# A gated-attention stage in another order of issue: context projection between the feed-forward's products, its norm ahead of the sum, one quarter of the squares on ScalarE

## The chip, the core and the metric

The kernel runs on one core of a Trainium2 chip. The metric is the device time of one execution in microseconds; the median of three runs is used. All data are fp32 except where bf16 is said.

## The reference, cut to what matters

The whole program is eight residual layers over `x` of shape 8 x 512 x 128. The change touches the stage between the fifth layer's attention and the seventh layer's attention. That stage computes, for each of the 8 batches:

```python
x = x + context @ W_o.T                      # end of the fifth layer
h = layernorm(x) @ W_fc' ; r = relu(h)**2    # sixth layer: 512 hidden columns, in 4 quarters
x = x + r @ W_proj'
n = layernorm(x)                             # seventh layer: gated attention, its inputs
q, k, v = n @ wq + bq, n @ wk + bk, n @ wv + bv
c = tanh(q @ wfq + bfq + mean(q) @ wfg + bfg)
p, z = c @ up, c @ uz                        # per head: position and steepness of a curve
```

The curve from `p` and `z`, and `q` and `k`, are split into three bf16 parts each and stored to DRAM, from where the seventh layer's attention loads them.

## The kernel before

The stage is the class `GatedPhase`. It is a software pipeline over 8 batches (`NB`), one batch per step, each batch spread over five steps: in step `s` the code works on batch `s` ("lag 0"), `s-1`, `s-2`, `s-3` and `s-4`. There is no scheduler at run time. Each engine has its own list, written out by hand in the methods `tensor`, `scalar`, `vector`, `vector_late` and `gpsimd`, executes it strictly in that order, and waits on semaphores where data come from another engine. `store` is the list of the DMA queue SP.

A batch goes this way. Lag 0: `out.project` (L173, TensorE), `out.add` (L179, VectorE adds it to `x`), `norm.statistics` and `aggregate_alone` (L213, L238, VectorE), `scale_alone` (L244, L247, GpSimd), `normalise_alone` (L254, VectorE), `norm.turn` (L269, transposes on TensorE), `norm.copy` (L275, ScalarE). Lag 1: `ffn.hidden` four times (L403, TensorE; the quarters in the order 2, 0, 3, 1), `ffn.relu` (L408, ScalarE) and `ffn.square` (L413) of each quarter, `ffn.project` (L421, 32 instructions on TensorE, which needs all four squares), `ffn.add` (L428, VectorE), then the second norm by the same lines as the first, `query` (L675), `key` (L679), `mix_query` (L692), `globals` (L730). Lag 2: `centre` (L725), `centre_tanh` (L743), `steepness` (L748), `value` (L684), `position` (L752), `values` (L719), and the splits of q and k into parts (`query_high`, `query_rest` L703, `middle` L452, `low` L456). Lag 3: `steep` (L759 exponential, L762 square, ScalarE), `position_tanh`, `distance`, `curves` (L779, L781, VectorE), `curves_high` (L786), `curves_rest` (L791). Lag 4: the last split of the curve (`c_split.low`, L456 with 1536 columns) and its stores (L1253 to L1259).

In the kernel before, squares 0 and 1 are on VectorE and squares 2 and 3 on GpSimd. GpSimd's list for step `s` holds `ffn.square(pool, s, ...)`, so it waits there for the relus of the next step.

PSUM has eight banks, and `Banks` gives each product one of them by a table; the entry of a table row is (name, bank, lag, semaphores of its readers). `take` makes TensorE wait until the bank's user before has been read. Before, `o` (the feed-forward's sum) and `out` (the context's) share bank 1, so `out.project` waits for `ffn.add` of the batch before.

In `last_group` further work is put between the steps: `rest.scale` on GpSimd in step 2 (L1428), and fills of the attention's operand stacks (L1571 on GpSimd, L1712 on VectorE, L1727 on ScalarE) with the attention's loads on SP (L1515) after steps 7, 8 and 10. TensorE leaves the stage after step 9 and enters the attention.

Of the kernel before, what the change touches and what calls it, by code (L numbers as in the profile page):

```python
# [11 lines left out]
ACT = mybir.ActivationFunctionType  # L12
# [74 lines left out]
def batch(s, lag):  # L87

    return (s - lag,) if 0 <= s - lag < NB else ()


class Banks:
# [4 lines left out]
    def __init__(self, nc, tag, count, plan, tensors=None, prior=None):  # L97
        self.tensors = tensors if tensors is not None else [nc.alloc_psum_tensor(f"{tag}_bank{i}", [P, 512], F32) for i in range(count)]
        self.prior = prior
        self.where = {name: bank for name, bank, _, _ in plan}  # L100
        self.readers = {name: readers for name, _, _, readers in plan}
        self.before, last = {}, {}
        uses = sorted((b + lag, k, name, bank, b) for k, (name, bank, lag, _) in enumerate(plan) for b in range(NB))
        for _, _, name, bank, b in uses:
            self.before[name, b] = last.get(bank)
            last[bank] = (name, b)
        self.last = last
# [54 lines left out]
class OutProjection:  # L162
# [6 lines left out]
    def project(self, pe, b):  # L169
        self.context.context_done(pe, b)  # L170
        to = self.banks.take(pe, "out", b)
        for t in range(NT):
            last = pe.matmul(to[:, t * D:(t + 1) * D], self.sv.ctxT[:, b, t * P:(t + 1) * P], self.wo, start=True, stop=True)  # L173
        last.then_inc(self.projected, 1)
# [213 lines left out]
class SquaredRelu:  # L388
# [21 lines left out]
    def square(self, eng, b, k):  # L410
        eng.wait_ge(self.relu_done[k], b + 1)
        r = self.r[b % 2][:, k, :]
        eng.tensor_tensor(r, r, r, ALU.mult).then_inc(self.sq_done[k], 1)  # L413

    def project(self, pe, b):
        for k in range(NK):
# [110 lines left out]
def x_tiles_of(tensor, b):  # L527

    return tensor[:, b * NT:(b + 1) * NT, :]
# [264 lines left out]
class PolarPhase:  # L794
# [44 lines left out]
    def tensor(self, pe, s):  # L839
        norm, norm2, ffn, prep = self.norm, self.norm2, self.ffn, self.prep  # L840
        for b in batch(s, 3):
            ffn.combine(pe, b)
        for b in batch(s, 4):
            norm2.turn(pe, b)
            prep.project(pe, b)
            prep.value(pe, b)
        for b in batch(s, 1):
            ffn.route(pe, b)
        for b in batch(s, 0):
            norm.turn(pe, b)  # L850
        for b in batch(s, 2):
            ffn.turn(pe, b)
        for b in batch(s, 1):
            ffn.low_rank(pe, b)
# [77 lines left out]
    def gpsimd(self, pool, s):  # L932
        norm, norm2, ffn, prep = self.norm, self.norm2, self.ffn, self.prep
        for b in batch(s, 5):
            norm2.scale(pool, b)
        for b in batch(s, 3):
            ffn.bias(pool, b)
        for b in batch(s, 0):
            norm.scale(pool, b)
# [151 lines left out]
class GatedPhase:  # L1091
# [4 lines left out]
    def __init__(self, nc, sv, tag, wo, early, late, psum, context):  # L1096
        self.sv = sv
        out = self.out = OutProjection(early, sv, f"{tag}_o", wo, context)
        ffn_norm = Norm(early, sv, f"{tag}_n", "xnT", out.added)
        ffn = self.ffn = SquaredRelu(early, sv, f"{tag}_f", ffn_norm, last_hidden=1)  # L1100
        norm, norm2 = self.norm, self.norm2 = ffn_norm, Norm(early, sv, f"{tag}_m", "xnT2")
        prep = self.prep = PrepareGated(late, sv, f"{tag}_p", norm2, early)
        norm2.x_ready = ffn.x_done
        self.place = (4, 5, 6, 7, 0, 1, 2, 3)
        banks = self.banks = Banks(nc, tag, 8, (
            ("h2", 4, 1, (ffn.relu_done[2],)), ("h0", 2, 1, (ffn.relu_done[0],)), ("h3", 5, 1, (ffn.relu_done[3],)), ("h1", 3, 1, (ffn.relu_done[1],)),
            ("c", 5, 2, (prep.cT_ready,)), ("o", 1, 1, (ffn.x_done,)), ("out", 1, 0, (out.added,)),
            ("z", 6, 2, (prep.ez_ready,)), ("v", 4, 2, (prep.v_ready,)), ("p", 7, 2, (prep.th_ready,)), ("xnT2", 0, 1, (norm2.xnT_ready,)),
            ("q", 2, 1, (prep.q_ready,)), ("xnT", 0, 0, (norm.xnT_ready,)), ("k", 3, 1, (prep.k_split.rest_ready,)), ("g", 5, 1, (prep.gb_ready,))), tensors=[psum[:, i, :] for i in self.place])
        out.banks = norm.banks = norm2.banks = ffn.banks = prep.banks = banks  # L1110

    def bank_done(self, eng, place):
# [22 lines left out]
    def tensor(self, pe, s):  # L1135
        out, norm, norm2, ffn, prep = self.out, self.norm, self.norm2, self.ffn, self.prep
        for b in batch(s, 1):
            ffn.hidden(pe, b, 2)
            ffn.hidden(pe, b, 0)
            ffn.hidden(pe, b, 3)  # L1140
            ffn.hidden(pe, b, 1)
        for b in batch(s, 2):
            prep.centre(pe, b)
        for b in batch(s, 1):
            ffn.project(pe, b)
        for b in batch(s, 0):
            out.project(pe, b)
        for b in batch(s, 2):
            prep.steepness(pe, b)
            prep.value(pe, b)  # L1150
            prep.position(pe, b)
        for b in batch(s, 1):
            norm2.turn(pe, b)
            prep.query(pe, b)
        for b in batch(s, 0):
            norm.turn(pe, b)
        for b in batch(s, 1):
            prep.key(pe, b)
            prep.globals(pe, b)

    def scalar(self, act, s):
        out, norm, norm2, ffn, prep = self.out, self.norm, self.norm2, self.ffn, self.prep
        for b in batch(s, 2):
            prep.query_high(act, b)
            prep.key_high(act, b)
        for b in batch(s, 3):
            prep.steep(act, b)
        for b in batch(s, 1):
            ffn.relu(act, b, 2)
            ffn.relu(act, b, 0)  # L1170
            ffn.relu(act, b, 3)
            ffn.relu(act, b, 1)
        for b in batch(s, 3):
            prep.position_tanh(act, b)
            prep.distance(act, b)
        for b in batch(s, 2):
            prep.centre_tanh(act, b)
            prep.q_split.middle(act, b)
            prep.k_split.middle(act, b)
        for b in batch(s, 3):  # L1180
            prep.curves_high(act, b)
        for b in batch(s, 4):
            prep.c_split.middle(act, b)
        for b in batch(s, 1):
            norm2.copy(act, b)
            prep.mix_query(act, b)
        for b in batch(s, 0):
            norm.copy(act, b)

    def vector_start(self, dve):  # L1190
        out, norm, norm2, ffn, prep = self.out, self.norm, self.norm2, self.ffn, self.prep
# [2 lines left out]
    def vector(self, dve, s):  # L1194
        out, norm, norm2, ffn, prep = self.out, self.norm, self.norm2, self.ffn, self.prep
        for b in batch(s, 2):
            prep.global_bias(dve, b)
            prep.key_rest(dve, b)
        for b in batch(s, 1):
            ffn.square(dve, b, 0)  # L1200
            ffn.square(dve, b, 1)
        for b in batch(s, 2):
            prep.query_rest(dve, b)
        for b in batch(s, 3):
            prep.curves(dve, b)
        for b in batch(s, 2):
            prep.q_split.low(dve, b)
            prep.k_split.low(dve, b)
        for b in batch(s, 1):
            ffn.add(dve, b)  # L1210
            norm2.statistics(dve, b)
            norm2.aggregate_alone(dve, b)
        for b in batch(s, 0):
            out.add(dve, b)
            norm.statistics(dve, b)
            norm.aggregate_alone(dve, b)
        for b in batch(s, 1):
            norm2.normalise_alone(dve, b)
        for b in batch(s, 2):
            prep.values(dve, b)  # L1220
        for b in batch(s, 0):
            norm.normalise_alone(dve, b)

    def vector_late(self, dve, s):
        prep = self.prep
# [4 lines left out]

    def gpsimd(self, pool, s):
        out, norm, norm2, ffn, prep = self.out, self.norm, self.norm2, self.ffn, self.prep
        for b in batch(s, 1):
            norm2.scale_alone(pool, b)
        for b in batch(s, 0):
            norm.scale_alone(pool, b)
            ffn.square(pool, b, 2)
            ffn.square(pool, b, 3)

    def store(self, sp, s):  # L1240
        sv, prep = self.sv, self.prep
# [1838 lines left out]
```

## Time and profile before

| | |
|---|---|
| median of 3 runs | 1714.1 us (1712.29 to 1714.25) |
| the profiled execution | 1712.71 us, its span 1710.9 us |
| busy over the span | PE 1504.7 us, DVE 1190.1, ACT 1257.0, POOL 530.2 |
| the gated stage | from 1111 us (first `out.project`) to 1300 us (the attention's reductions run without a stop) |
| one steady step of it | 18.33 us |
| TensorE's granted clock, mean | 0.95 of full speed |

PE is TensorE's matmuls, PEld its weight loads, DVE VectorE, ACT ScalarE, POOL GpSimd, SP the queue of transfers. L numbers are lines of the kernel. PEclk is the granted TensorE clock as a share of 2.4 GHz. In a timeline, a line's start minus the start of the line before it on the same engine is what the instruction occupies when the engine does not wait; the duration shown is some 0.1 us longer, since the next instruction starts before the last one's results are all written.

### The profile page before, as it was taken

How to read it: one execution, taken by the hardware profiler on the slowest of the kernel's cores; microseconds unless marked ns; L12 is line 12 of the kernel's file. 1: busy time of each engine (PE TensorE's matmuls, PEld its weight loads, DVE VectorE, ACT ScalarE, POOL GpSimd, SP SyncE). 2: the span in 40 equal slices, each digit the busy share in tenths (PEclk: the TensorE clock that was granted, in tenths of full speed). 3: DMA queues.
4: the chain of work that ended last, by engine and by line, in shares of the span. 5: the costliest groups of instructions: out<-in, count | busy, mean ns of one | idle time of the engine just before them, and what ended most of it. 6: DMA issues, size and time to landing. Idle time of an engine off the chain costs nothing. (4 is left out here: it accounts for less than half of the span.)

```text
span 1710.9 us, 37885 instructions
## 1 busy us (share of the span) xinstructions
PE 1504.7 (88%) x14142; PEld 724.0 (42%) x14142; DVE 1190.1 (70%) x1933; ACT 1257.0 (73%) x2113; POOL 530.2 (31%) x908
## 2 busy tenths in 40 slices
PE   7889987774699999998889999978874999999998
PEld 4666666662133333336633333345541333333356
DVE  4778777798999999967710000047878999999743
ACT  4654563697488888885689999926663888888863
POOL 3422342552323333334400010022221333333362
PEclk9999998797699999999999999989986999999999
DMA  4000000025434444420133333211333333333211
GB/s 132 1 1 2 1 2 1 1 82 166 142 102 111 107 110 111 107 62 27 45 89 98 94 100 97 66 36 39 99 108 113 84 91 89 89 92 92 67 38 38
DMA packets 140411, 125.42 MB, mean 73 GB/s; under 512 B 38411, under 2 KB 118341, under 8 KB 140229
## 3 DMA queue, kind: packets, MB, share of 16 engines
q1 hardware_dynamic: 130980, 121.90, 24.6%
q0 software_dynamic: 8192, 0.77, 0.9%
q8 instruction: 113, 1.85, 0.5%
q14 instruction: 70, 0.57, 0.1%
q10 hardware_dynamic: 1056, 0.33, 0.1%
HBM read 77.19 MB, written 44.96 MB: 71 GB/s over the span
## 5 line engine op out<-in xcount | busy, mean ns | idle before, releaser
L1700 ACT ACTIVATE m_probs<-m_psum 128x512 f32<-128x512 f32 (+1 forms) x768 | 511.6, 761 | 60.9 <-PE m_psum L1623 59.9
L1700 ACT ACTIVATE e_probs<-e_psum 128x512 f32<-128x512 f32 x512 | 276.4, 596 | 53.6 <-PE e_psum L1623 52.0
L1740 DVE TENSOR_REDUCE a_minus_max<-m_psum 128x2 f32<-128x1024 f32 x256 | 300.8, 1218 | 14.4 <-PE m_psum L1632 13.1
L1740 DVE TENSOR_REDUCE a_minus_max<-e_psum 128x2 f32<-128x1024 f32 x256 | 300.5, 1218 | 14.8 <-PE e_psum L1632 13.3
L1623 PE MATMUL m_psum<-m_q_stack,m_k_stack 114*32 114x512 bf16 (+1 forms) x4096 | 294.3, 384 | 6.6 <-DMA m_k_stack<-n_parts 4.4
L1643 PE MATMUL m_psum<-m_probs,m_v_ones 128*32 128x512 f32 x2048 | 269.5, 599 | 3.9 <-DVE m_pair L1690 2.6
L1623 PEld LDWEIGHTS m_psum<-m_q_stack,m_k_stack 114*32 114x32 bf16 (+1 forms) x4096 | 106.4, 96 | 224.2 <-issue 124.6
L1623 PE MATMUL e_psum<-e_q_stack,e_k_stack 126*32 126x512 bf16 x2048 | 157.5, 384 | 2.3 <-ACT e_probs L1700 2.2
L1643 PE MATMUL e_psum<-e_probs,e_v_ones 128*32 128x512 f32 x1024 | 132.2, 593 | 0.0
L1632 PE MATMUL m_psum<-m_k_stack,m_q_stack 48*128 48x512 bf16 x512 | 93.2, 400 | 31.8 <-DVE a_minus_max L1740 24.3
L1632 PE MATMUL e_psum<-e_k_stack,e_q_stack 60*128 60x512 bf16 x512 | 93.9, 400 | 29.4 <-DVE a_minus_max L1740 23.6
L1583 POOL CAST a_max_parts<-a_minus_max 128x16 bf16<-128x16 f32 x64 | 12.7, 198 | 325.2 <-DVE a_minus_max L1740 325.2
L1522 POOL DMA_DIRECT2D m_q_stack<-a_max_rows x128 | 76.6, 604 | 58.5 <-DVE a_max_rows L1745 51.3
L1522 POOL DMA_DIRECT2D e_q_stack<-a_max_rows x128 | 76.4, 603 | 57.8 <-DVE a_max_rows L1745 50.8
L1623 PEld LDWEIGHTS e_psum<-e_q_stack,e_k_stack 126*32 126x32 bf16 x2048 | 43.8, 95 | 117.1 <-ACT e_probs L1700 70.0
L1962 POOL TENSOR_TENSOR s_rope_product<-s_qkv,rope 128x512 f32<-128x512 f32 x32 | 40.2, 1287 | 152.3 <-ACT s_qkv L1927 152.3
L1643 PEld LDWEIGHTS m_psum<-m_probs,m_v_ones 128*32 128x32 f32 x2048 | 52.4, 109 | 78.9 <-ACT m_probs L1700 53.2
L1577 POOL COPY m_v_ones<-vtok 128x128 f32<-128x128 f32 x64 | 18.6, 292 | 213.2 <-PE m_psum L1643 213.2
L1690 DVE COPY slot_w<-m_psum 128x512 f32<-128x512 f32 x8 | 5.5, 691 | 111.8 <-PE m_psum L1643 111.8
L1413 DVE RECIPROCAL slot_wo<-slot_wo 128x64 f32<-128x64 f32 x24 | 13.1, 546 | 91.1 <-DMA slot_wo<-a_context_pairs 91.1
L1632 PEld LDWEIGHTS m_psum<-m_k_stack,m_q_stack 48*128 48x128 bf16 x512 | 24.6, 93 | 114.5 <-issue 53.3
L1632 PEld LDWEIGHTS e_psum<-e_k_stack,e_q_stack 60*128 60x128 bf16 x512 | 24.5, 93 | 114.3 <-DVE a_minus_max L1740 53.8
(402 smaller groups left out, 2630.3 us busy)
## 6 DMA issues: line engine op xcount, KB each, us to landing
polar_q<-m_late SPq DMA_DIRECT2D x24, 256.0 KB, 3.0
polar_k<-m_late SPq DMA_DIRECT2D x24, 256.0 KB, 3.2
m_q_stack<-polar_q SPq DMA_DIRECT2D x64, 96.0 KB, 2.3
m_k_stack<-polar_k SPq DMA_DIRECT2D x64, 96.0 KB, 2.4
ctx<-a_context_pairs SPq DMA_DIRECT2D x48, 128.0 KB
a_context_pairs<-slot_w SPq DMA_DIRECT2D x24, 256.0 KB, 2.2
m_q_stack<-dist_parts SPq DMA_DIRECT2D x192, 32.0 KB
m_k_stack<-dist_parts SPq DMA_DIRECT2D x192, 32.0 KB
```

What stands on the lines that cost most here:

```text
L1413: dve.reciprocal(self.inverse, self.sums).then_inc(self.inverted, 1)
L1522: pool.dma_start(rows[:, :, j:j + 32], self.max_rows[j:j + 32, :]).then_inc(self.rows_loaded, 16)
L1577: pool.tensor_copy(self.buf.v_ones[n % 2][:, :, :, DH * (n % 2):DH * (n % 2) + DH], self.sv.vtok[:, tiles_of(b), :].rearrange("p t (h d) - ...
L1583: pool.tensor_copy(self.max_parts[:, 0, :], self.minus_max[n % 2][:, :]).then_inc(self.hi_ready, 1)
L1623: last = pe.matmul(self.ps_s[i % self.PAIRS][r:r + 32, j, :], self.buf.k_stack[g][0:self.rows, h, c * P + r:c * P + r + 32], self.buf.q_st ...
L1632: pe.matmul(to[:, :], self.buf.q_stack[g][part, h, t * P:(t + 1) * P], self.buf.k_stack[g][part, h, :], start=True, stop=True).then_inc(se ...
L1643: last = pe.matmul(self.ps_pv[32 * h:32 * h + self.buf.VW, :], self.buf.v_ones[m % 2][:, c, h, :], self.buf.probs[(NT * m + c) % self.buf. ...
L1690: copied = eng.tensor_copy(self.buf.pair[k % 2][:, :], self.ps_pv[:, :])
L1700: act.activation(self.buf.probs[(NT * m + c) % self.buf.PROBS][:, self.WIDE * part:self.WIDE * (part + 1), :], self.ps_s[i % self.PAIRS], ...
L1740: dve.tensor_reduce(self.minus_max[n % 2][:, k:k + NT + 1:NT], self.ps_r[r % self.TWOS], AX.X, ALU.max, negate=True).then_inc(self.two_fre ...
L1962: pool.tensor_tensor(self.products[n][:, :, :, :], halves[:, :, :, i, :], table, ALU.mult).then_inc(self.rope_steps, 1)
```

## The change

`out` moves to bank 0, which it shares with `xnT` and `xnT2`; `o` has bank 1 alone. TensorE issues `out.project` (batch s) between `ffn.hidden` and `centre`, and `norm.turn` (batch s) directly after `ffn.project`. VectorE issues `out.add`, its statistics and its aggregation directly after its squares, `normalise_alone` of that norm after `curves`, hence ahead of `ffn.add`; `k_split.low` and `values` go behind the second norm's aggregation. Square 3 moves from GpSimd to VectorE, square 2 to ScalarE; GpSimd keeps the norms' scales alone. ScalarE issues `steep` behind its third relu and `norm.copy` ahead of `norm2.copy`.

```diff
+    def square_beside(self, act, b, k):
+        act.wait_ge(self.relu_done[k], b + 1)
+        r = self.r[b % 2][:, k, :]
+        act.activation(r, r, ACT.Square).then_inc(self.sq_done[k], 1)
...
-            ("c", 5, 2, (prep.cT_ready,)), ("o", 1, 1, (ffn.x_done,)), ("out", 1, 0, (out.added,)),
+            ("out", 0, 0, (out.added,)), ("c", 5, 2, (prep.cT_ready,)), ("o", 1, 1, (ffn.x_done,)), ("xnT", 0, 0, (norm.xnT_ready,)),
...
-            ("q", 2, 1, (prep.q_ready,)), ("xnT", 0, 0, (norm.xnT_ready,)), ("k", 3, 1, (prep.k_split.rest_ready,)), ("g", 5, 1, (prep.gb_ready,))), tensors=[psum[:, i, :] for i in self.place])
+            ("q", 2, 1, (prep.q_ready,)), ("k", 3, 1, (prep.k_split.rest_ready,)), ("g", 5, 1, (prep.gb_ready,))), tensors=[psum[:, i, :] for i in self.place])
...
@@ tensor
             ffn.hidden(pe, b, 1)
+        for b in batch(s, 0):
+            out.project(pe, b)
         for b in batch(s, 2):
             prep.centre(pe, b)
         for b in batch(s, 1):
             ffn.project(pe, b)
         for b in batch(s, 0):
-            out.project(pe, b)
+            norm.turn(pe, b)
...
-        for b in batch(s, 0):
-            norm.turn(pe, b)
-        for b in batch(s, 1):
             prep.key(pe, b)
...
@@ scalar
+        for b in batch(s, 1):
+            ffn.relu(act, b, 2)
+            ffn.relu(act, b, 0)
+            ffn.square_beside(act, b, 2)
+            ffn.relu(act, b, 3)
         for b in batch(s, 3):
             prep.steep(act, b)
         for b in batch(s, 1):
-            ffn.relu(act, b, 2)
-            ffn.relu(act, b, 0)
-            ffn.relu(act, b, 3)
             ffn.relu(act, b, 1)
...
+        for b in batch(s, 0):
+            norm.copy(act, b)
         for b in batch(s, 1):
             norm2.copy(act, b)
             prep.mix_query(act, b)
-        for b in batch(s, 0):
-            norm.copy(act, b)
@@ vector
             ffn.square(dve, b, 0)
+            ffn.square(dve, b, 3)
             ffn.square(dve, b, 1)
+        for b in batch(s, 0):
+            out.add(dve, b)
+            norm.statistics(dve, b)
+            norm.aggregate_alone(dve, b)
         for b in batch(s, 2):
             prep.query_rest(dve, b)
         for b in batch(s, 3):
             prep.curves(dve, b)
+        for b in batch(s, 0):
+            norm.normalise_alone(dve, b)
         for b in batch(s, 2):
             prep.q_split.low(dve, b)
-            prep.k_split.low(dve, b)
         for b in batch(s, 1):
             ffn.add(dve, b)
             norm2.statistics(dve, b)
             norm2.aggregate_alone(dve, b)
-        for b in batch(s, 0):
-            out.add(dve, b)
-            norm.statistics(dve, b)
-            norm.aggregate_alone(dve, b)
+        for b in batch(s, 2):
+            prep.k_split.low(dve, b)
+            prep.values(dve, b)
         for b in batch(s, 1):
             norm2.normalise_alone(dve, b)
-        for b in batch(s, 2):
-            prep.values(dve, b)
-        for b in batch(s, 0):
-            norm.normalise_alone(dve, b)
@@ gpsimd
+        for b in batch(s, 0):
+            norm.scale_alone(pool, b)
         for b in batch(s, 1):
             norm2.scale_alone(pool, b)
-        for b in batch(s, 0):
-            norm.scale_alone(pool, b)
-            ffn.square(pool, b, 2)
-            ffn.square(pool, b, 3)
```

## Rows read from the trace of the kernel before

**Rows 1.** Busy time by stretch: gated stage, step 0 to 1, 1 to 2, one steady step.
```profile
core 0: us, PE busy (x) PEld busy (x) DVE busy (x) ACT busy (x) POOL busy (x), PEclk, DMA share, GB/s
1130.60:1150.25 19.65, 15.22 (x64) 9.45 (x64) 10.75 (x35) 8.57 (x14) 4.61 (x6) 0.83 0.05 16
1205.43:1223.76 18.33, 15.68 (x76) 9.84 (x76) 16.19 (x39) 12.01 (x20) 5.02 (x6) 1.00 0.32 93
```

**Rows 2.** Timeline, TensorE, one steady step: start, us, engine, line, operation, [idle before <- releaser].
```profile
1194.86 3.70 PE L403 MATMUL e_psum<-e_v_ones,ffn_fc 128*128 128x512 f32 x8
1200.84 3.81 PE L421 MATMUL e_psum<-ffn_proj,e_probs 128*128 128x128 f32 x32 [0.99 <-DVE e_probs L413]
1205.43 1.16 PE L173 MATMUL e_psum<-l1a_wo,ctx 128*128 128x128 f32 x8 [0.78 <-DVE x L428]
1206.42 1.02 PE L748 MATMUL e_psum<-e_probs,l1b_up 128*128 128x512 f32 x2
1209.04 0.98 PE L269 MATMUL e_psum<-ident,e_q_stack 128*128 128x128 f32 x4
1210.71 1.13 PE L675 MATMUL e_psum<-e_k_stack,l1b_w 128*128 128x512 f32 x2 [0.69 <-ACT e_k_stack L275]
1213.19 3.70 PE L403 MATMUL e_psum<-e_k_stack,ffn_fc 128*128 128x512 f32 x8
```

**Rows 3.** Timeline, VectorE, the same step.
```profile
1200.66 0.68 DVE L703 SCALAR_TENSOR_TENSOR e_late<-pope_table,e_late 128x512 f32<-128x512 f32 x1
1201.26 0.68 DVE L779 TENSOR_TENSOR e_late<-e_late 128x512 f32<-128x512 f32 x1
1202.58 1.28 DVE L456 TENSOR_TENSOR e_late<-e_late 128x512 bf16<-128x512 f32 x2
1204.68 0.69 DVE L428 TENSOR_TENSOR x<-e_psum,x 128x512 f32<-128x512 f32 x1 [0.81 <-PE e_psum L421]
1205.41 0.87 DVE L213 BATCH_NORM_STATS2 e_pair<-x 128x6 f32<-128x128 f32 x4
1206.32 0.38 DVE L238 BATCH_NORM_AGGREGATE e_pair<-e_pair 128x2 f32<-128x6 f32 x4
1208.55 1.08 DVE L254 TENSOR_SCALAR e_q_stack<-x,e_pair 128x128 f32<-128x128 f32 x4
1209.56 0.68 DVE L719 TENSOR_TENSOR vtok<-e_psum,bv 128x512 f32<-128x512 f32 x1
```

**Rows 4.** Timeline, ScalarE and GpSimd, the same step.
```profile
1195.78 0.61 ACT L759 ACTIVATE e_late<-e_psum 128x512 f32<-128x512 f32 x1
1196.42 0.72 ACT L762 ACTIVATE e_late<-e_late 128x512 f32<-128x512 f32 x1
1197.05 2.14 ACT L408 ACTIVATE e_probs<-e_psum 128x512 f32<-128x512 f32 x4
...
1207.10 1.04 POOL L247 TENSOR_TENSOR e_pair<-e_pair,minus_half 128x4 f32<-128x4 f32 x1
```

**Rows 5.** Timeline, PE and ACT, step 2, where ScalarE waits for the first product.
```profile
1140.44 3.68 PE L403 MATMUL e_psum<-e_v_ones,ffn_fc 128*128 128x512 f32 x8
1141.58 0.60 ACT L408 ACTIVATE e_probs<-e_psum 128x512 f32<-128x512 f32 x1 [0.39 <-PE e_psum L403]
```

**Rows 6.** All instructions of line 413: ns min/median/max, first and last start.
```profile
L413 DVE TENSOR_TENSOR e_probs<-e_probs x16: 692/1144/1522, 1123.0 to 1255.2; 128x512 f32<-128x512 f32 x16
```

**Rows 7.** Timeline at the stage's end: a normalisation beside a fill, a gap of TensorE.
```profile
1264.18 1.52 DVE L254 TENSOR_SCALAR e_q_stack<-x,e_pair 128x128 f32<-128x128 f32 x4 [1.48 <-POOL e_pair L247]
1265.28 0.81 PE L269 MATMUL e_psum<-ident,e_q_stack 128*128 128x128 f32 x4 [2.01 <-DVE e_q_stack L254]
```

**Rows 8.** Chain of work that ended last, at the stage's end: start, us, what.
```profile
1268.57 1.68 DVE e_late L456
1270.27 0.52 SPq L1253
...
1289.30 0.59 SPq L1259
```

## The prediction

> **What bounds the kernel now.** I read the busy time by stretch first. The change touches one stage, 1111 to 1300 us, so only that stretch counts. In a steady step no engine is full: TensorE is busy 15.7 us of 18.33, VectorE 16.2, ScalarE 12.0, GpSimd 5.0, and the clock is at its upper level, 2.4 GHz [rows 1]. So the step is not paced by one engine's load but by a loop of waits through several. Next I read the timelines of one step, engine by engine [rows 2 to 4], for the instructions that stood idle and who released them, and added the links into a loop:
>
> the four hidden products start at 1194.86; the sum `ffn.project` starts 5.98 us later, when the last square is done; 3.84 us later VectorE adds it to x (1204.68); then 0.73 for the add and 0.91 for the statistics; from the aggregation (1206.32) to the second norm's normalisation (1208.55) 2.23; 2.16 from there through transposes and copy to `query` (1210.71); 2.48 through `norm.turn`, `key` and `globals` to the next hidden products (1213.19) [rows 2, 3]. Sum: 5.98 + 3.84 + 0.73 + 0.91 + 2.23 + 2.16 + 2.48 = 18.33, the whole step. Every link is on the path; what lengthens one lengthens the step. TensorE waits in this loop 0.99, 0.78 and 0.69 us [rows 2]; these gaps are what a new order could win.
>
> Within the 2.23, the other batch's `out.add`, statistics and aggregation stand between the aggregation and the normalisation. GpSimd's result is there earlier: its second instruction ends at 1207.10 + 1.04 = 1208.14, 1.82 after the aggregation began [rows 3, 4].
>
> **The change, part by part.** All times count from the first hidden product of a step. I use what an instruction occupies (start to next start): an add from PSUM 0.73, statistics 0.91, aggregation 0.30, `query_rest` 0.60, both `curves` 1.32, four normalisations 1.01, `values`, a `low` or an uncontended square 0.61 [rows 3]; a hidden product 0.86 (3.70 for four, with the last one's tail) [rows 2]; relus 0.51 apart, 0.60 long; exponential 0.64; Square from SBUF 0.63 [rows 4].
>
> *The square on ScalarE, and `steep` behind relu 3.* ScalarE's first relu starts at 1.14 where ScalarE is free [rows 5], and it will be, since `steep` (1.27) no longer precedes it. Relu 0 follows at 2.00, the square at 2.51, relu 3 at 3.14, exponential 3.65, Square 4.29, relu 1 at 4.92, done 5.52. Before, relu 1 was the fourth of the group that starts at 1197.05: 2.19 + 3 x 0.51 = 3.72 [rows 2, 4]. So the last relu comes 1.20 later. The new square is not in the trace; its nearest row is L762, the same function from and to SBUF, 0.63. Queued behind it are relu 3, `steep` and relu 1; relu 1 waits anyway, VectorE waits for relu 1.
>
> *The squares on VectorE.* With GpSimd squaring beside them, VectorE's squares take 1.14 in the median and up to 1.52; the shortest is 0.69 [rows 6]. GpSimd's list loses its squares, so I take 0.61 occupied each. Three cost 1.83 where two cost 2.6. But quarter 1 sets the end: 5.52 + 0.03, done 6.24; `ffn.project` starts at 6.33 against 5.98: **+0.35**. `out.project` (0.99) and `centre` (0.86) lie ahead of it, ending at 3.44 + 0.99 + 0.86 = 5.29, under that wait, and cost nothing.
>
> The Trainium skill, "SBUF — State Buffer", section "Who interferes with whom", says that a VectorE instruction with two SBUF inputs and a GpSimd one that reads SBUF exclude each other. It would price the three squares as I do; without it, at 1.14 each, the sum would be some 1.5 us a step more.
>
> *The pile ahead of `ffn.add`.* VectorE leaves square 1 at 6.16 and then issues, in strict order: `out.add` 0.73, statistics 0.91, aggregation 0.30, `query_rest` 0.60, `curves` 1.32, `normalise_alone` 1.01, `q_split.low` 0.61. That is 5.48, so it is free at 11.64. GpSimd's scale (7.80 + 1.82) is ready before `normalise_alone` at 10.02 and adds nothing. The feed-forward's sum is ready at 6.33 + 3.84 = 10.17. Before, VectorE did 3.2 us of work in this window and still waited 0.81 [rows 3]; now `ffn.add` is late by **+1.47**. Behind it wait the second norm, `query`, `key` and the next step.
>
> *The second norm.* With nothing of the other batch between, normalisation starts 1.85 after the aggregation instead of 2.23: **-0.38**. `k_split.low` and `values` (1.22) fit into 1.85 - 0.30 = 1.55. `value` is done on TensorE before 13.5, `values` is due at 14.2.
>
> *`norm.turn` away from between `query` and `key`.* It frees TensorE 0.43, but `globals` waits for `mix_query`'s sum, so the 2.48 shrinks to between 2.25 and 2.48; I take 2.30: **-0.18**. The turn itself lies in TensorE's new idle time.
>
> *Banks.* `out` no longer waits for `ffn.add`, so the 0.78 gap goes. In bank 0, `out`, `xnT` and `xnT2` follow each other with some us to spare.
>
> One steady step: 18.33 + 0.35 + 1.47 - 0.38 - 0.18 = **19.6 us, +1.26**. Bounds 19.5 and 19.8 by the 2.30.
>
> **The sum.** Steps 3 to 7 (five hidden-to-hidden intervals with `steep` and `curves`): 5 x 1.26 = +6.3. Step 2 has neither: last relu 3.72, square 4.35, aggregation at 6.60, normalisation, held by GpSimd, 8.45, `ffn.add` at 10.07 where the sum is ready at 5.29 + 3.84 = 9.13: +0.94 - 0.38 - 0.18, about +0.4. Step 1 runs partly at half clock (0.83 in its stretch [rows 1]), where the turn between `query` and `key` costs double, 0.86: -0.5, between -0.9 and 0. Step 8 has no lag-0 work, so no pile: `values` slips into the 1.48 that VectorE waits for GpSimd there [rows 7], -0.6, and faster squares give up to 0.6 more: -0.95. What ends this stage is SP's queue, which issues from the end of `c_split.low` of step 8 (1270.27) without a stop until 1289.9 [rows 8]; the attention follows it, so the shift at that `low` is the shift of the end.
>
> GpSimd, without squares to wait for, runs `rest.scale` (step 2) and the fill of stack 0 (step 7) directly behind the second norm's scale, beside the normalisation on the loop. A fill there made a normalisation 1.52 instead of 1.08 [rows 7, 3]: +0.44 for the fill; for `rest.scale` between that and the 0.83 by which a square was stretched at most [rows 6]. Together +1.0. SP's load of stack 0 goes out earlier, into idle time of its queue, and SP's stores of k come later, still before 1270: nothing.
>
> Total: 6.3 + 0.4 - 0.5 - 0.95 + 1.0 = +6.25 us, on the profiled execution's 1712.71 us (1710.9 us of span and 1.8 around it). The median of the runs is 1.4 above that execution; the same shift gives 1714.1 + 6.25 = **1720.3 us**. Ends of the terms: +4.7 and +8.6; with a margin for a start-to-start here and there, 1717.5 to 1723.5.
>
> **The rivals.** *A, the pile is covered (not slower).* If what VectorE does between square 1 and `ffn.add` fits under the 3.84 of the sum, the add is not late: step 18.33 + 0.35 - 0.38 - 0.18 = 18.12, five of them -1.05, step 2 -0.55, edges and GpSimd -0.45 to -1: about 1712. It decides at a pile of 4.0 us; the rows give 5.48, which speaks against it. For it: adjacent independent VectorE instructions might overlap more than I count. 0.15, with partial forms up to 1717.
>
> *B, engine load paces the step (faster).* VectorE falls to 16.2 - 2.6 + 1.8 = 15.4 us and TensorE has 15.7; at 15.7 a step, five steps give -13: about 1701. Against it: the loop above explains 18.33 exactly, with 2 us idle on VectorE. 0.04. The Trainium skill, "Perfetto Trace Analysis", section "Identifying the Most-Contended Engine", says to relieve the engine of highest occupancy, which here is VectorE beside TensorE; by it the change would pay.
>
> *C, the clock falls (slower still).* TensorE's idle share grows from 2.65 to 3.9 us a step, most of it in one place: some 1.4 us before `norm2.turn`, then 0.69 before `query`. Before, gaps of 2.01 us [rows 7] and more stood ahead of stretches at 1.2 GHz; the steady step's, up to 0.99, did not. If it falls there, `query` and `key` run at half speed, about +1.9 us each time; in two to six steps +4 to +11: 1724 to 1732. For: two gaps close together. Against: each is under 2.01. 0.15.
>
> **From these to the numbers.** Forecast 0.66, A 0.15, B 0.04, C 0.15. A measurement of this kernel tells 0.2% (3.4 us) from no change. Range for eight in ten: 1713.5 to 1728, into A and C. Slower by over 0.2% (above 1717.5): 0.71, the forecast but for its low end, and C. Within: 0.20. Faster: 0.09, B and A's far end.
>
> **What would show it.** After: step period 19.6; relu 1 starts 4.9 after the hidden products; squares 0.69 long; `ffn.add` released by nothing on TensorE (no idle before it), 1.5 after the sum is ready; a TensorE gap of 1.4 before the second transposes; VectorE idle over 1 us before square 1. Wrong if `ffn.add` still waits for L421, if the step is under 18.6, or if PEclk in the steps is under 1.00.

## The result, and the profile after

The changed kernel takes 1737.4 us in the median of 4 runs (1734.4 to 1738.7) against 1714.2 for the kernel before (4 runs): ratio 1.012, 95% interval 1.010 to 1.014. It is slower by 23 us, where the forecast was 6.

The profiled execution took 1738.45 us, 25.7 more than that of before. The stage, from its first `out.project` to the attention's uninterrupted reductions, grew from 1299.67 - 1111.58 = 188.1 us to 1325.54 - 1116.57 = 209.0: +20.9. The other 5 us lie before the stage, at code that the change doesn't touch; the stage of the ten other kernels below, whose code ahead of it is the same, began anywhere between 1110.0 and 1119.2, so I count that part as scatter. I compare stages from here on, each read from one profiled execution.

By part of the stage: up to the first hidden products +0.9; step 1 21.84 against 21.87; step 2 21.33 against 17.58, +3.75; the five steps 3 to 7 109.36 against 91.90, **+17.5**, which is 21.87 a step against 18.38; all behind them 48.53 against 49.75, -1.2. Sum 20.9.

Windows of the kernel after, step 2 and two steady steps; they answer to [rows 1].

```profile
core 0: us, PE busy (x) PEld busy (x) DVE busy (x) ACT busy (x) POOL busy (x), PEclk, DMA share, GB/s
1146.32:1167.65 21.33, 17.60 (x77) 10.79 (x78) 12.21 (x35) 9.16 (x15) 4.46 (x5) 0.90 0.14 38
1211.53:1232.78 21.25, 17.40 (x77) 10.57 (x78) 15.90 (x39) 12.66 (x20) 3.51 (x4) 0.91 0.27 79
1232.78:1254.52 21.74, 17.88 (x79) 10.73 (x78) 15.91 (x39) 12.97 (x22) 3.51 (x4) 0.88 0.29 82
```

The clock column tells most: 1.00 before, 0.88 to 0.91 now. VectorE's work fell from 16.2 to 15.9 us (rival B counted 15.4), ScalarE's rose from 12.0 to 12.7 and 13.0 with the square that it took over, GpSimd lost 1.5 us, and yet the mean step is 3.5 us longer. TensorE's busy time rose from 15.7 to 17.4 and 17.9 us for about the same instructions: they run slower.

Timeline of TensorE in the step from 1232.78 (answers to [rows 2]).

```profile
1232.78 3.68 PE L403 MATMUL e_psum<-e_k_stack,ffn_fc 128*128 128x512 f32 x8
1238.94 3.81 PE L426 MATMUL e_psum<-ffn_proj,e_probs 128*128 128x128 f32 x32 [0.72 <-issue]
1248.82 1.16 PE L269 MATMUL e_psum<-ident,e_q_stack 128*128 128x128 f32 x4 [1.83 <-DVE e_q_stack L254]
1250.66 2.07 PE L680 MATMUL e_psum<-e_k_stack,l1b_w 128*128 128x512 f32 x2 [0.69 <-ACT e_k_stack L275]
1252.53 1.91 PE L684 MATMUL e_psum<-e_k_stack,l1b_w 128*128 128x512 f32 x2
1254.52 1.20 PE L403 MATMUL e_psum<-e_v_ones,ffn_fc 128*128 128x512 f32 x1
```

Windows of TensorE alone behind the two gaps: busy, clock.

```profile
core 0: us, PE busy (x), PEclk, DMA share, GB/s
1250.00:1252.50 2.50, 1.83 (x2) 0.50 0.66 183
1252.50:1254.50 2.00, 2.00 (x5) 0.50 0.24 47
```

`query` took 1.13 before and takes 2.07 now; `key` and the first hidden product are slow too. The granted clock is 0.50 there, 1.2 GHz. Two gaps lie ahead, 1.83 and 0.69 us, with the transposes between.

Timeline of VectorE and GpSimd in the same step (answers to [rows 3, 4]).

```profile
1238.15 0.69 DVE L413 TENSOR_TENSOR e_probs<-e_probs 128x512 f32<-128x512 f32 x1 [1.03 <-ACT e_probs L408]
1242.87 1.12 DVE L254 TENSOR_SCALAR e_q_stack<-x,e_pair 128x128 f32<-128x128 f32 x4 [0.21 <-POOL e_pair L247]
1244.51 0.68 DVE L433 TENSOR_TENSOR x<-e_psum,x 128x512 f32<-128x512 f32 x1
1246.13 0.38 DVE L238 BATCH_NORM_AGGREGATE e_pair<-e_pair 128x2 f32<-128x6 f32 x4
1246.43 0.66 DVE L461 TENSOR_TENSOR e_late<-e_late 128x512 bf16<-128x512 f32 x1
1246.60 0.57 POOL L244 TENSOR_SCALAR e_pair<-e_pair 128x4 f32<-128x4 f32 x1 [3.76 <-DVE e_pair L238]
1247.26 1.04 POOL L247 TENSOR_TENSOR e_pair<-e_pair,minus_half 128x4 f32<-128x4 f32 x1
1248.33 1.12 DVE L254 TENSOR_SCALAR e_q_stack<-x,e_pair 128x128 f32<-128x128 f32 x4 [0.64 <-POOL e_pair L247]
```

Square 1 (L413) starts at 5.37 of the step (forecast 5.55) and `ffn.add` (L433) at 11.73 (forecast 11.64), with no idle time before it: the pile is about as forecast, though VectorE waits 0.21 in it for GpSimd's scale of the first norm (L254 at 1242.87), which the forecast put at nothing. But the second normalisation starts 2.20 after the aggregation instead of 1.85. GpSimd's L244 takes 0.57 where it takes 0.23 with nothing of this kind beside it, and beside it runs `k_split.low` (L461), which has two inputs in SBUF.

Timeline in step 2.

```profile
1160.81 1.26 POOL L1433 TENSOR_TENSOR ctx<-ctx,e_scale 128x512 f32<-128x512 f32 x1
1160.87 2.05 DVE L254 TENSOR_SCALAR e_q_stack<-x,e_pair 128x128 f32<-128x128 f32 x4 [0.64 <-POOL e_pair L247]
1162.30 1.01 PE L269 MATMUL e_psum<-ident,e_q_stack 128*128 128x128 f32 x4 [2.77 <-DVE e_q_stack L254]
1164.00 2.06 PE L680 MATMUL e_psum<-e_k_stack,l1b_w 128*128 128x512 f32 x2 [0.69 <-ACT e_k_stack L275]
```

The normalisation beside `rest.scale` (L1433) takes 2.05 us instead of 1.1, the gap on TensorE is 2.77, and the clock falls here too.

### The profile page after: what moved, and what is told of

Read it like the earlier page. It is cut to its first block and busy times, and to the rows that moved or that the text cites. A ratio compares the mean times of both kernels' runs of the same rounds, so it can differ in the third digit from the quotient of the medians.

```text
span 1736.7 us, 37886 instructions
## 1 busy us (share of the span) xinstructions
PE 1522.8 (88%) x14142; PEld 732.0 (42%) x14142; DVE 1189.1 (68%) x1941; ACT 1263.3 (73%) x2121; POOL 516.6 (30%) x892
## 3 DMA queue, kind: packets, MB, share of 16 engines
q8 instruction: 113, 1.85, 0.5%
## 5 line engine op out<-in xcount | busy, mean ns | idle before, releaser
L1588 POOL CAST a_max_parts<-a_minus_max 128x16 bf16<-128x16 f32 x64 | 12.7, 198 | 324.3 <-DVE a_minus_max L1745 324.3
```

## The experiments

Theory: the dependences are those of the forecast, and two prices were wrong. The clock falls once a step behind the new gap (about 1.9 us a step), and `k_split.low` holds GpSimd up (0.35). Rival: the order itself is longer than I counted, and the slow products are only its sign. Stages are given against the 188.1 of before. The kernel before had medians of 1717.1 us (11 runs) beside experiments 1 to 4, 1715.7 (29 runs) beside 5 to 8, and 1716.8 (9 runs) beside 9 and 10.

### 1. The gap filled

Two products, whose result nobody reads, in the gap ahead of `norm2.turn`:

```diff
+            prep.keep_busy(pe, b)     # 2 products, fp32, 512 columns, bank of key
             norm2.turn(pe, b)
             prep.query(pe, b)
```

> The changed kernel, with two extra fp32 products of 512 columns (constants by constants, into the bank that key overwrites later) on TensorE between position and the second norm's transposes, where it idles 1.8 us. They leave the result alone. Theory (the fall of the clock is a cost of its own, caused by the idle stretch before query): with TensorE kept busy there, the granted clock stays at 1.00 from step 2 on, query to the next hidden products takes 2.3 us instead of 3.86, the step 20.0 us instead of 21.7, and the kernel is 10 to 14 us faster than the changed one, some 1724 us. Rival (the order of the waits alone makes the step long; the clock only shows it): the step stays at 21.5 us or more, the kernel at 1735 or more.

Measured: 1726.2 us, ratio 1.0051 (1.0030 to 1.0072); stage 197.4, +9.3. Timeline of TensorE, and the step's window:

```profile
1216.94 1.88 PE L685 MATMUL e_psum<-ffn_fc,l1b_w 128*128 128x512 f32 x4
1218.93 1.00 PE L269 MATMUL e_psum<-ident,e_q_stack 128*128 128x128 f32 x4
1220.62 1.12 PE L680 MATMUL e_psum<-e_k_stack,l1b_w 128*128 128x512 f32 x2 [0.69 <-ACT e_k_stack L275]
1222.86 0.68 PE L403 MATMUL e_psum<-e_k_stack,ffn_fc 128*128 128x512 f32 x1
...
1202.91:1222.86 19.95, 17.81 (x82) 10.63 (x82) 15.89 (x40) 12.74 (x21) 3.51 (x4) 1.00 0.29 85
```

Added work (L685) makes the kernel 11 us faster: the clock is 1.00, `query` 1.12, and `query` to the next hidden products 2.24 (forecast 2.30). The step falls to 19.96. Apart from the two products the order is that of after, so over half of the loss is the clock.

One part of the expectation was missed: the clock did not hold from step 2 on. In step 2, with `rest.scale` beside the normalisation, a gap of 1.05 us was left behind the dummy products, `query` took 1.75, and the step was 21.51 us, no shorter than the 21.33 of after.

### 2. `values` ahead of `k_split.low`

```diff
-            prep.k_split.low(dve, b)
             prep.values(dve, b)
+            prep.k_split.low(dve, b)
```

> The changed kernel, with values ahead of k_split.low on VectorE, so that the instruction beside GpSimd's first scale instruction has one input in SBUF instead of two. Theory (VectorE's two-input instruction holds GpSimd up): GpSimd's L244 behind the second aggregation takes 0.23 us instead of 0.57, the normalisation starts 1.85 to 1.95 us after the aggregation instead of 2.20, the step is 0.3 us shorter, the kernel 1.5 to 2.5 us faster, if the clock goes on falling. Rival (GpSimd is slow for another reason, or VectorE then waits for value): 2.2 us as before, kernel within 1 us.

Measured: 1733.6 us, 1.0087 (1.0065 to 1.0110); stage 206.7, 2.3 less than after. Timeline:

```profile
1200.96 0.38 DVE L238 BATCH_NORM_AGGREGATE e_pair<-e_pair 128x2 f32<-128x6 f32 x4
1201.26 0.66 DVE L724 TENSOR_TENSOR vtok<-e_psum,bv 128x512 f32<-128x512 f32 x1
1201.43 0.23 POOL L244 TENSOR_SCALAR e_pair<-e_pair 128x4 f32<-128x4 f32 x1 [3.76 <-DVE e_pair L238]
1202.81 1.12 DVE L254 TENSOR_SCALAR e_q_stack<-x,e_pair 128x128 f32<-128x128 f32 x4 [0.29 <-POOL e_pair L247]
```

With an instruction beside it whose first input is in PSUM (L724), L244 takes 0.23 again and the normalisation starts 1.85 after the aggregation, as I had forecast. The same two instructions in the other order are worth 0.35 us a step.

### 3. The last relu ahead of `steep`

```diff
             ffn.relu(act, b, 3)
+            ffn.relu(act, b, 1)
         for b in batch(s, 3):
             prep.steep(act, b)
```

> The changed kernel, with steep put back behind the last relu on ScalarE. Theory (the delayed last relu starts the pile on VectorE late, one for one): relu 1 starts 3.7 us after the hidden products instead of 4.76, square 1, out.add and ffn.add come about 1.0 to 1.2 earlier, the step is 1.0 to 1.2 us shorter; the kernel is 6 us faster, some 1731, if the clock still falls in each step, and some 1720 if it holds. Rival (the late relu is hidden, the pile alone counts): under 2 us.

Measured: 1729.2 us, 1.0064 (1.0045 to 1.0084); stage 198.9, 10.1 less than after, more than I expected. The clock still falls once a step; timeline:

```profile
1224.18 1.00 PE L269 MATMUL e_psum<-ident,e_q_stack 128*128 128x128 f32 x4 [1.82 <-DVE e_q_stack L254]
1225.87 1.84 PE L680 MATMUL e_psum<-e_k_stack,l1b_w 128*128 128x512 f32 x2 [0.69 <-ACT e_k_stack L275]
```

The step is 20.4. Experiment 6 repeats this with the clock held.

### 4. An order of my own

Experiment 3, and the batches' norms apart: `ffn.add` and its statistics come first on VectorE, then the other batch's `normalise_alone`; both lows go behind the second normalisation; `norm.turn` goes behind `position`, with `xnT` in bank 1.

VectorE's part of the edit, without the `for` lines:

```diff
-            norm.normalise_alone(dve, b)
-            prep.q_split.low(dve, b)
             ffn.add(dve, b)
             norm2.statistics(dve, b)
             norm2.aggregate_alone(dve, b)
-            prep.k_split.low(dve, b)
+            norm.normalise_alone(dve, b)
             prep.values(dve, b)
             norm2.normalise_alone(dve, b)
+            prep.q_split.low(dve, b)
+            prep.k_split.low(dve, b)
```

> A version of my own from the same parts: the squares and out.project as in the changed kernel; steep behind the last relu; normalise_alone of the first norm moved behind ffn.add and its aggregation, beside GpSimd's scale; both lows behind the second normalisation; norm.turn behind position, its bank is bank 1. The pile ahead of ffn.add is then 0.61 + 1.94 + 0.60 + 1.32 = 4.47 from square 1 at 4.33, so VectorE is free at 8.80, and the sum is ready at 5.29 + 3.84 = 9.13: ffn.add is not late. Theory (pile, late relu and clock are the whole loss): step 9.13 + 1.64 + 1.95 + 2.16 + 2.3 = 17.2 us, clock 1.00, kernel 5 to 8 us faster than before the change, 1706 to 1709. Rival (another wait takes the place, or the clock falls in the new gaps too): 1714 or more.

Measured: **1711.2 us, 0.9957 (0.9942 to 0.9973)**: faster than both kernels; stage 180.0, -8.1. Timeline and window:

```profile
1205.75 0.69 DVE L433 TENSOR_TENSOR x<-e_psum,x 128x512 f32<-128x512 f32 x1 [0.17 <-PE e_psum L426]
1209.28 1.11 DVE L254 TENSOR_SCALAR e_q_stack<-x,e_pair 128x128 f32<-128x128 f32 x4
1209.77 1.01 PE L269 MATMUL e_psum<-ident,e_q_stack 128*128 128x128 f32 x4 [0.62 <-DVE e_q_stack L254]
...
1196.71:1213.70 16.99, 15.68 (x79) 9.91 (x78) 15.63 (x40) 12.97 (x21) 3.16 (x4) 1.00 0.34 100
```

`ffn.add` (L433) waits for TensorE's sum again, so the pile is gone; the gap ahead of the second transposes is 0.62 and the clock stays at 1.00. The step is 16.99 with about the same work on every engine as in the changed kernel.

### 5. Experiments 1 and 2 together

> The changed kernel with both corrections at once: two dummy products (fp32, 512 columns, into the bank of key) in the gap ahead of the second transposes, and values ahead of k_split.low. Theory (the clock's fall and GpSimd held up by k_split.low are the two terms that I had wrong): the two misses add up, so the steady step is 21.87 - 1.9 - 0.36 = 19.6 us, the step of my blind forecast; granted clock 1.00 in the steps; GpSimd's L244 0.23 instead of 0.57; query to the next hidden products 2.2; the stage about 195 us, the kernel about 2 us under the one with the dummies alone (1726), so 1724. Rival (the second norm isn't on the path once the clock holds, because the dummies or k_split.low behind it delay the step instead): the step stays at 20.0 and the kernel at 1726.

Measured: 1724.4 us, 1.0048 (1.0033 to 1.0064); stage 195.2, +7.1. One steady step:

```profile
1219.99:1239.61 19.62, 17.58 (x82) 10.64 (x82) 15.91 (x40) 12.76 (x21) 3.16 (x4) 1.00 0.29 86
```

With both wrong prices put right the steady step is 19.62, where the forecast said 19.6, and the kernel is 8.7 us over that of before. The rival of the theory above, a longer order than I counted, falls.

### 6. Experiments 1 and 3 together

> The changed kernel with the dummy products and with the steep pair behind the last relu instead of ahead of it. It takes the late relu away with the clock held. Theory (the late relu delays square 1, and with it everything of the pile, by 1.2 us less what else ends the wait): square 1 starts at 4.3 instead of 5.4 after the first hidden product, ffn.add at 10.5 instead of 11.7, step 18.7 to 18.9, stage about 191 to 192 us, kernel about 1720; clock 1.00. Rival (the pile is bound by something else, such as out.project's sum or GpSimd's scale, or the exponential and the Square then come late for curves): ffn.add comes no more than 0.4 earlier, step 19.6 or more, kernel 1724.

Measured: 1718.3 us, 1.0011 (0.9998 to 1.0024); stage 191.6, +3.5.

```profile
1201.72:1220.67 18.95, 17.58 (x83) 10.69 (x82) 15.90 (x40) 12.87 (x21) 3.51 (x4) 1.00 0.31 90
```

`ffn.add` starts at 1212.42 - 1201.72 = 10.70 instead of 11.73 and the step is 1.0 shorter than in experiment 1 (19.96). So the late relu, with `steep` ahead of it, is worth 1.0 us a step: it pushes out everything that VectorE does before `ffn.add`.

### 7. The squares alone, in the kernel before

```diff
             ffn.relu(act, b, 0)
+            ffn.square_beside(act, b, 2)
             ffn.relu(act, b, 3)
...
             ffn.square(dve, b, 0)
+            ffn.square(dve, b, 3)
             ffn.square(dve, b, 1)
...
-            ffn.square(pool, b, 2)
-            ffn.square(pool, b, 3)
```

> The kernel before with the squares alone moved: ScalarE squares quarter 2 behind relu 0, VectorE squares 0, 3 and 1, GpSimd none; the order of everything else is that of before. Theory (uncontended squares take 0.69 instead of 1.14, three cost VectorE 1.83 where two cost 2.6, so square 1 ends about 0.2 to 0.5 earlier although ScalarE's last relu comes 0.5 later): ffn.project starts at 5.5 to 5.8 instead of 5.98, the steady step is 18.0 to 18.2 instead of 18.38, total -1 to -2.5 us. Rival (the later last relu, 4.2 instead of 3.7, is what square 1 then waits for, and VectorE's third square pushes out query_rest and the curves against GpSimd and the store of the lows): the step is 18.4 to 18.8, total +0 to +2.

Measured (12 runs): 1713.1 us, 0.9980 (0.9966 to 0.9994); stage 186.1, -2.0. Timeline:

```profile
1194.67 3.70 PE L403 MATMUL e_psum<-e_v_ones,ffn_fc 128*128 128x512 f32 x8
1198.97 1.29 DVE L413 TENSOR_TENSOR e_probs<-e_probs 128x512 f32<-128x512 f32 x2 [0.31 <-ACT e_probs L408]
1200.37 3.81 PE L426 MATMUL e_psum<-ffn_proj,e_probs 128*128 128x128 f32 x32 [0.19 <-DVE e_probs L413]
```

`ffn.project` starts 5.70 into the step instead of 5.98, and the step is 18.05. In the order of before, this part of the change gains a little; the loss comes with the new order.

### 8. Experiment 4 with the first two steps filled

```diff
+            if b < 2:
+                prep.keep_busy(pe, b, 2 - b)
             norm.turn(pe, b)
```

> The order of the fourth experiment with dummy products ahead of the first transposes in the first two steps only (two for batch 0, one for batch 1), where there is no value, steepness or position yet and TensorE idles longest. Theory (those two steps, 20.9 and 18.2 us against 17.0 for the later ones, are long partly because the clock has fallen in the idle time before): steps 1 and 2 together 2 to 4 us shorter, PEclk 0.97 or more there, kernel 2 to 4 us under the fourth experiment on the same chip, that is 1707 to 1709. Rival (those steps are long because batch 0 and 1 wait for the attention's last results and the engines' lists, not for the clock): within 1 us of the fourth experiment.

Measured: 1707.8 us, 0.9950 (0.9933 to 0.9966); stage 179.8 against 180.0. Step 1 fell from 20.86 to 19.30, but step 2 rose from 18.18 to 18.95, its clock down from 0.98 to 0.93, and step 3 from 16.99 to 17.33. Most of what one step gained the next two gave back. The intervals of experiments 4 and 8 overlap, so the outcome is the rival's. Its reason isn't: step 1 did get shorter when TensorE was kept busy.

### 9. `rest.scale` moved, in experiment 5

```diff
+                    if s == 3:                    # between the two norms' scales
+                        rest.scale(pool, NB - 1, 0, 1)
...
-                    if s == 2:                    # behind both
-                        rest.scale(pool, NB - 1, 0, 1)
```

> The fifth experiment (dummy products, values first) with GpSimd's rest.scale (a product of 128x512) moved from directly behind the second norm's scale of the second step to between the two norms' scales of the third, where GpSimd stands idle for some 3 us. Theory (beside rest.scale the second normalisation of step 2 takes 2.05 us instead of 1.1, and the gap that this opens on TensorE is what lets the clock fall there): step 2 is 20.9 - 0.9 = 19.9 us from the longer normalisation alone, and 1.3 less again if the clock then holds, so 18.5 to 18.7; the normalisation 1.1 long; the other steps 19.6; kernel 2 us under the fifth experiment's 1724. Rival (the normalisation is long for another reason, or the step's clock falls all the same): step 2 at 20.0 to 20.9, kernel within 1 us.

Measured: 1724.5 us, 1.0045 (1.0028 to 1.0062); stage 194.8, not clearly less than the 195.2 of experiment 5. Step 2 went from 20.86 to 19.01, but step 3 from 20.17 to 21.88. Timeline and a window of step 3:

```profile
1172.71 1.27 POOL L1440 TENSOR_TENSOR ctx<-ctx,e_scale 128x512 f32<-128x512 f32 x1
1172.78 2.05 DVE L254 TENSOR_SCALAR e_q_stack<-x,e_pair 128x128 f32<-128x128 f32 x4 [0.21 <-POOL e_pair L247]
1174.21 1.00 PE L269 MATMUL e_psum<-ident,e_q_stack 128*128 128x128 f32 x4 [1.55 <-DVE e_q_stack L254]
...
1176.00:1178.00 2.00, 2.00 (x10) 0.50 0.02 4
```

I had moved it from beside one normalisation to beside the other: the same 2.05 us, a gap of 1.55 on TensorE, and the clock at 0.50 some 2 us later. The longer normalisation beside `rest.scale` is shown in two places, and the cure failed.

### 10. The same move in experiment 8

There the first norm's normalisation comes much later than its scale, so the new place has no normalisation beside it.

> The eighth experiment (own order, dummy products in the first two steps) with the same move of rest.scale. Theory: step 2, 18.95 there, comes to 17.0 to 17.4, since the normalisation is 0.9 shorter and no gap over 1 us is left ahead of the second transposes; kernel 1 to 2 us under the eighth experiment, about 1706 on a chip where the kernel before gives 1715.7. Rival: the clock falls in step 2 or 3 all the same, and the kernel stays at 1707 to 1708.

Measured: **1705.5 us, 0.9933 (0.9911 to 0.9954)**; stage 178.6, -9.5. Timeline of step 2:

```profile
1149.71 1.11 DVE L254 TENSOR_SCALAR e_q_stack<-x,e_pair 128x128 f32<-128x128 f32 x4
1154.12 3.68 PE L403 MATMUL e_psum<-e_k_stack,ffn_fc 128*128 128x512 f32 x8
```

The normalisation takes 1.11, and step 2, from 1137.14 to 1154.12, is 16.98 us long, 1.2 less than in experiment 4. By its median and its stage this is the fastest of the twelve kernels, but its interval overlaps those of experiments 4 and 8.

## Why the prediction was wrong

**The step that failed** is the weighing of rival C. I forecast a gap of "some 1.4 us before `norm2.turn`, then 0.69 before `query`", and then wrote "Against: each is under 2.01", and gave it 0.15. The gaps came as forecast in four of the five steady steps (1.83 with the held-up GpSimd, 1.48 without it in experiment 2, and 0.69; in the fifth, where the fill of stack 0 runs beside the normalisation, 2.43), and the clock fell in every steady step, in experiment 2 as well. With the fall, "2.48 shrinks to between 2.25 and 2.48; I take 2.30: -0.18" became 3.86. Experiment 1 prices the fall: 21.87 - 19.96 = 1.9 us a step, the 1.9 that rival C names. My mistake was to compare single gaps with one gap of before. The new order puts two of them close together, around a short piece of work. That their sum is what counts isn't shown: behind 1.48 + 0.69 in experiment 2 the clock fell, behind 1.51 + 0.69 in step 2 of experiment 4 it held. I also counted "two to six steps"; it was all of them, and the rival's 1724 to 1732 was too low since other terms were low too.

**A term mis-sized: the second norm, -0.38.** It measured -0.03 (2.20 against 2.23). The first norm's scale was held up too, where I had written that it "adds nothing": 0.21 of waiting. I had taken GpSimd's two instructions from a place where nothing with two SBUF inputs ran beside them, and put `k_split.low` there without pricing it. The Trainium skill, "SBUF — State Buffer", section "Who interferes with whom", which I used for the squares, says the same of any VectorE instruction with two SBUF inputs; experiment 2 agrees, 0.57 against 0.23.

**A term mis-sized: step 2.** Forecast +0.4 and some 0.6 for `rest.scale`, measured +3.75. `ffn.add` came at 10.73 instead of 10.07, since GpSimd was held up in the first norm as well; the second norm took 2.20 instead of 1.85; from normalisation to `query` 3.13 instead of 2.16, of which 0.94 is the longer normalisation; and `query` to the next hidden products 3.65 instead of 2.30, at half clock. Experiments 9 and 10 take the normalisation's length away and get 1.85 and, against experiment 8, 18.95 - 16.98 = 1.97 back in that step.

**The sum again.** Measured +20.9 in the stage against +6.25. Steps 3 to 7: 17.5 against 6.3 + 0.44, so 10.7 more: about 9.5 the clock (5 x 1.9), 1.7 the second norm (5 x 0.34), the rest -0.5. Step 2: 2.75 more. Step 1: 0.5 more, and the way to it 0.9, where `out.project` ran at half clock (2.04 against 1.13). The end: 0.3 less. Together 14.6. The median's remaining 2.4 us are within the scatter from before the stage.

**What held.** The late relu and `ffn.project`: forecast start 6.33, measured 6.16. The pile: `ffn.add` at 11.64 against 11.73; from the end of square 1 (5.37 + 0.61) that is 5.75 of pile where 5.48 was counted, so the close hit is in part two small misses that cancel. That the pile decides above 4.0 us was right: in experiment 6, with the early relu, the sum is ready at 5.27 + 3.84 = 9.11 and `ffn.add` comes at 10.70; in experiment 4, with the pile cut, it comes at 9.04, and the kernel is faster than both. Uncontended squares at 0.69 and ScalarE's Square at 0.62. The end of the stage: -0.95 against -1.2. `ffn.add` late by 1.7 instead of 1.47. Experiment 5 gives back the blind step, 19.62 for 19.6.

**Rivals A and B.** A falls: the pile took 5.75 us, more than was counted. B falls too: VectorE's load fell from 16.2 to 15.9 us a step and the step grew. The Trainium skill, "Perfetto Trace Analysis", section "Identifying the Most-Contended Engine", would relieve that engine; here the same load took 21.7 us in one order and 17.0 in another.

## What to carry to other kernels

Where an order makes TensorE wait, price the wait twice: its own length, and the products behind it at half clock; and read the clock column of the windows first when the result comes. A single gap that the trace of before shows to be harmless says little about two that come close together; these runs don't give a rule for which pair is harmless. And when a small GpSimd instruction is on the path, choose what VectorE runs beside it; the same two instructions in the other order were worth 0.35 us a step.

## What the runs showed of the hardware

- The clock is not a function of one gap's length. It fell behind 1.83 + 0.69 us in four steady steps after and behind 2.43 + 0.69 in the fifth (`query` 1.72 to 2.08 us long in each, 1.13 at full clock), behind 1.55 in step 3 of experiment 9, and behind 0.71 + 0.69 in step 2 of experiment 5 (0.56 in its last 2.5 us). It held behind 0.62 + 0.69 in every steady step of experiment 4, and `query` ran at full speed (1.12) behind 1.51 + 0.69 in step 2 of the same kernel. Behind 2.01 + 0.69 at the stage's end `query` took 2.07 in the kernel before and 1.12 in experiment 7, where the clock fell only some 5 us later, behind further idle time. What decides between these stays open; that filling the gap holds the clock in the steady steps is shown by experiment 1.
- Two products in TensorE's idle time, 1.9 us a step together, bought 11 us.
- A 128x512 product of GpSimd (1.26 us) beside VectorE's four normalisations lengthens these from 1.1 to 2.05 us, in step 2 of the kernel after and of experiment 5, and in step 3 of experiment 9; where it is moved away (step 2 of experiments 9 and 10) they take 1.1. The Trainium skill, "SBUF — State Buffer", section "Who interferes with whom", says of tensor_scalar that it can take the port pair shared with GpSimd, and that the other is then blocked whole; the 0.94 added are some three quarters of one such product, so these rows agree in kind and not in full.
